# Projections and self-attention as one program: head loads in the last projection steps, fills in free banks

## The reference

```python
q = _ln(latents, sa_ln_g, sa_ln_b)
x = latents + _mha(q, q, sa_in_w, sa_in_b, sa_out_w, sa_out_b)
qc = _ln(x, ca_q_ln_g, ca_q_ln_b)
kv = _ln(tokens, ca_kv_ln_g, ca_kv_ln_b)
x = x + _mha(qc, kv, ca_in_w, ca_in_b, ca_out_w, ca_out_b)
return _fuse_moe(x, moe_ln_g, moe_ln_b, router_w, router_b, e_fc1_w, e_fc1_b, e_fc2_w, e_fc2_b)
...
scores = jnp.einsum('bhqd,bhkd->bhqk', q, k) / jnp.sqrt(jnp.float32(dh))
attn = jax.nn.softmax(scores, axis=-1)
out = jnp.einsum('bhqk,bhkd->bhqd', attn, v)
```

## Time and profile before

| | |
|---|---|
| median of three runs | 1690.89 us (1687.65 to 1694.73) |
| profiled execution | 1686.37 us, span of its trace 1684.6 us |
| projections | 0 to about 139 us |
| self-attention | about 139 to 829 us |
| busy share of the span | PE 86%, DVE 70%, ACT 50%, POOL 44% |

### The profile page before, as it was taken

The page is one execution under the profiler, slowest core; times in us unless marked ns, Lnnn a source line. Parts: engine busy times, 40 slices in busy tenths (PEclk is TensorE's granted clock), DMA queues, the critical chain, the costliest instruction groups (busy, mean ns, idle before and its releaser), DMA issues. The chain is left out here.

```text
span 1684.6 us, 29075 instructions
## 1 busy us (share of the span) xinstructions
PE 1441.5 (86%) x9973; PEld 745.6 (44%) x9974; DVE 1181.5 (70%) x1725; ACT 844.1 (50%) x1709; POOL 743.7 (44%) x465
## 2 busy tenths in 40 slices
PE   5993999999999999999658888873299999999996
PEld 3550222222222222222233544442288888888885
DVE  4755999999999999997165777434655665655653
ACT  2330788888888888888414545340022222222221
POOL 1003999999930000000131221100158887888884
PEclk8995899999999999999876979565599999999999
DMA  3556645574522111200264665535722332333331
GB/s 119 188 212 177 163 132 153 156 215 134 157 57 84 32 32 33 84 1 2 89 142 105 163 140 98 121 73 191 297 42 55 56 55 48 53 60 54 54 57 16
DMA packets 134790, 172.68 MB, mean 103 GB/s; under 512 B 30008, under 2 KB 100089, under 8 KB 134187
## 3 DMA queue, kind: packets, MB, share of 16 engines
q1 hardware_dynamic: 107499, 119.26, 26.6%
q0 software_dynamic: 27200, 52.24, 12.9%
HBM read 102.09 MB, written 66.25 MB: 100 GB/s over the span
## 5 line engine op out<-in xcount | busy, mean ns | idle before, releaser
L1093 DVE TENSOR_REDUCE sa_half_maxs<-sa_psm 128x2 f32<-128x1024 f32 x512 | 604.7, 1221 | 49.7 <-PE sa_psm L961 41.2
L1077 ACT ACTIVATE sa_p<-sa_pss 128x512 f32<-128x512 f32 x1024 | 533.0, 603 | 89.8 <-PE sa_pss L1004 89.6
L1004 PE MATMUL sa_pss<-sa_q,sa_k 49*128 49x512 f16 x1024 | 312.2, 385 | 7.8
L1019 PE MATMUL sa_pso<-sa_p,sa_v 128*32 128x512 f32 x2048 | 273.8, 606 | 18.8 <-ACT sa_o L1055 9.4
L961 PE MATMUL sa_psm<-sa_k,sa_q 48*128 48x512 f16 x1024 | 260.9, 395 | 30.5 <-DMA sa_k<-dram_sa_qk_parts 19.2
L2295 ACT ACTIVATE moe_h<-moe_psh,moe_b 128x256 f32<-128x256 f32 x312 | 122.4, 475 | 328.4 <-PE moe_psh L2232 328.4
L1004 PEld LDWEIGHTS sa_pss<-sa_q,sa_k 49*128 49x128 f16 x1024 | 77.7, 94 | 320.2 <-ACT sa_p L1077 264.9
L1366 POOL TENSOR_TENSOR x_xb<-x_xb,early_bo 128x1024 f32<-128x1024 f32 x4 | 9.4, 2350 | 373.4 <-DMA x_xb<-in_x 373.4
L2231 PE MATMUL moe_psh<-moe_hl,w_high 128*128 128x256 f16 x624 | 171.0, 274 | 0.0
L2230 PE MATMUL moe_psh<-moe_hh,w_high 128*128 128x256 f16 x624 | 170.9, 274 | 0.0
L2232 PE MATMUL moe_psh<-moe_hh,w_low 128*128 128x256 f16 x624 | 170.9, 274 | 0.0
(11 more groups left out here) (205 smaller groups left out, 2026.2 us busy)
## 6 DMA issues: line engine op xcount, KB each, us to landing
sa_w_stage<-in_w POOLq DMA_DIRECT2D x32, 512.0 KB, 5.3
dram_sa_v<-qkv_v_sb SPq DMA_DIRECT2D x8, 1024.0 KB, 5.0
dram_sa_qk_parts<-qkv_part SPq DMA_DIRECT2D x16, 512.0 KB, 6.0
sa_v<-dram_sa_v SPq DMA_DIRECT2D x16, 512.0 KB, 6.5
dram_w_high<-sa_w_high POOLq DMA_DIRECT2D x32, 256.0 KB, 2.8
dram_w_low<-sa_w_low POOLq DMA_DIRECT2D x32, 256.0 KB, 3.6
dram_sa_raw<-sa_o SPq DMA_DIRECT2D x4, 2048.0 KB, 9.1
w_high<-dram_w_high SPq DMA_DIRECT2D x16, 512.0 KB, 14.9
```

What stands on the lines that cost most here:

```text
L1004: pe.matmul(ps_s[place % SBANKS][:], k_st[u][rows, j0 + j, kt * kp:(kt + 1) * kp], q_st[u][rows, j0 + j, half * HALF:(half + 1) * HALF], s ...
L1019: mm = pe.matmul(ps_o[h * VW:(h + 1) * VW, :], v_st[u][:, kt, v_at:v_at + VW], probs[n % PSLOTS][h][:], start=(kt == 0), stop=(kt == key_t ...
L1077: act.activation(probs[n % PSLOTS][h][:], ps_s[place % SBANKS][:], ACT.Exp, scale=float(DH) ** -0.5).then_inc(read, 1)
L1093: dv.tensor_reduce(half_maxs[U % 2][:, at % 2, :, c], ps_m[z][:], AX_X, ALU.max).then_inc(taken, 1)
```

## The change

Projections and self-attention become one block (`front_phase`) with one set of semaphores. The buffers of loads 0 and 1 lie outside the memory that the projections give back; those of loads 2 and 3, the probabilities and the outputs are put in that memory later. SP issues load 0 in step 7 of the x program, behind the stores of block 5, and load 1 in step 8, behind those of block 6; in step 7 it first waits for the stores of blocks 0 and 1, the rows of the first batch. The bank pairs are laid out so that fill 0 goes to the pair that the projections leave free, and fill 1 to the pair of the transposes. When SP has seen all stores of a program land, it raises `over`; PE waits for it ahead of the first turn, ACT ahead of the first exponential, and GpSimd ahead of its first weight piece.

```diff
--- before.py
+++ after.py
@@ -346,6 +347,14 @@
                     sp.dma_start(qk[2][n].rearrange("(c p) n -> p c n", p=P)[
                         :, :, bass.ds(number(i, u) * W, W)], part[n][u][:]
                     ).then_inc(parts_stored[u], 16)
+            if ahead and has(0) and not has(1):
+
+                for u in range(2):
+                    sp.wait_ge(parts_stored[u], 16 * PARTS)
+                    sp.wait_ge(v_stored[u], 16)
+                ahead(sp, 0)
+            if ahead and has(-1) and not has(0):
+                ahead(sp, 1)
         steps(sp, step)
...
+        sp.sem_inc(over, 1)
...
-def tokens_phase(nc, *programs):
...
+def front_phase(nc, early, programs, q_parts, k_parts, v_dram, **attention):
+
+    slots, load_heads, key_tiles = 4, HG, SEQ // P
...
+        heads = [head_buffers(sb, u) for u in range(2)]
...
+        def load(sp, L):
+
+            u = L % slots
+            q_st, k_st, v_st = heads[u]
...
+        block = ctx.enter_context(nc.Block())
+        with ExitStack() as tctx:
+            psum = {"read": {}}
+            made = [tokens_program(nc, tctx, sem, block, psum, *args, **options, over=over,
+                                   ahead=load if n == len(programs) - 1 else None)
+                    for n, (args, options) in enumerate(programs)]
             for stage in range(2):
                 for program in made:
                     next(program, None)
+        with ExitStack() as actx:
...
+            heads += [head_buffers(late, u) for u in range(2, slots)]
+            attention_program(nc, actx, sem, block, "sa", heads, load, loaded, v_loaded, half_maxs, maxs, max_row,
+                              over, len(programs), early=early, **attention)
...
-        ps_s = [ps(f"pss{z}", [kp, HALF]) for z in range(SBANKS)]
-        ps_m = [ps(f"psm{z}", [P, 2, 512]) for z in range(2)]
-        ps_o = ps("pso", [P, HALF])
...
+    ps_m1 = ps("psm1", [P, 2, 512])
+    ps_s = [ps(f"pss{z}", [kp, HALF]) for z in range(SBANKS)]
+    ps_o = ps("pso", [P, HALF])
+    ps_m = [ps("psm0", [P, 2, 512]), ps_m1]
...
-                sp.dma_start(ident[:], ident_dram).then_inc(consts, 16)
-                load(0)
-                for u in range(slots):
...
-                load(1)
-                place_row(0)
...
+        pool.wait_ge(over, programs)
+        pool.wait_ge(filled, 1)
...
+        for n in range(lead):
+            advance(n)
+            if n == fills:
+                pe.wait_ge(consts, 16)
+                pe.wait_ge(over, programs)
+                turn(0)
...
+        keep_row(0)
+        act.wait_ge(over, programs)
```

More of the change, by code:

```diff
@@ L60, in semaphores, with tokens_program @@
     nc.all_engine_barrier()
-def tokens_program(nc, ctx, block, psum, name, x_dram, rows, blocks, *, ln_g, ln_b, ident_dram,
-                   attn=None, qk=None, v=None, router=None, weights=None):
+def tokens_program(nc, ctx, make_sem, block, psum, name, x_dram, rows, blocks, *, ln_g, ln_b, ident_dram,
+                   attn=None, qk=None, v=None, router=None, weights=None, ahead=None, over=None):
     W = TPB * rows
@@ L657, in early_buffers, with attention_program @@
     return made
-def attention_phase(nc, name, q_parts, k_parts, v_dram, raw_dram, ident_dram, ones_dram, weights, w_cut, early,
-                    a, ck_parts, cv_dram, r1):
+def attention_program(nc, ctx, sem, block, name, heads, load, loaded, v_loaded, half_maxs, maxs, max_row, over,
+                      programs, early, raw_dram, ident_dram, ones_dram, weights, w_cut, a, ck_parts, cv_dram, r1):
     keys = SEQ
@@ new lines, in attention_program @@
+    taken = sem("taken")
+    joined = sem("joined")
+    row_placed = [sem(f"row_placed{z}") for z in range(2)]
+    in_bank = sem("in_bank")
+    read = sem("read")
+    weighted = sem("weighted")
+    o_taken = sem("o_taken")
+    stored = [sem(f"stored{e}") for e in range(2)]
+    w_loaded = [sem(f"w_loaded{z}") for z in range(STAGES)]
+    w_highs = sem("w_highs")
+    w_scaled = sem("w_scaled")
+    w_lows = sem("w_lows")
+    w_stored = [sem(f"w_stored{z}") for z in range(2)]
+    sums_loaded = [sem(f"sums_loaded{b}") for b in range(BATCH - 1)]
@@ new lines, in attention_program, with home, period @@
+    recip_ready, recip_stored = sem("recip_ready"), sem("recip_stored")
+    early_consts, early_x, early_o = sem("early_consts"), sem("early_x"), sem("early_o")
+    EARLY = 16 * (13 + 2 * len(K_STACK) + 2)
+    first_recip = 2 * (batch_groups + 1) * fills + lead
+    LOADS = 16 * 2 * 2 * len(Q_STACK)
+    STORES = 16
+    def home(G):
+        L, g = divmod(G, groups_per_load)
+        return L % slots, g * PAIRS, L // slots
+    def period(n):
+        G, bt = divmod(n, per_group)
+        half, kt = divmod(bt, key_tiles)
+        return G, half, kt
@@ new lines, in _, with take, join @@
+    @block.vector
+    def _(dv):
+        def take(n):
+            U, f = divmod(n, fills)
+            z = n % 2
+            dv.wait_ge(filled, n + 1)
+            j, at = divmod(f, q_tiles)
+            c = j * q_tiles // 2 + at // 2
+            dv.tensor_reduce(half_maxs[U % 2][:, at % 2, :, c], ps_m[z][:], AX_X, ALU.max
+                             ).then_inc(taken, 1)
+        def join(U):
+            dv.wait_ge(taken, (U + 1) * fills)
+            if U >= 2:
+                dv.wait_ge(in_bank, row_place(U - 2) + 1)
+            dv.tensor_tensor(maxs[U % 2][:], half_maxs[U % 2][:, 0], half_maxs[U % 2][:, 1],
+                             ALU.max).then_inc(joined, 1)
+        for n in range(all_fills + 1):
+            U, f = divmod(n, fills)
+            if f == 0 and n > 0:
+                join(U - 1)
+            if n < all_fills:
+                take(n)
+            if n == first_recip:
+                dv.wait_ge(sums_loaded[0], 16)
+                dv.reciprocal(early["recips1"][:, 0, :], early["sums1"][:, 0, :]).then_inc(recip_ready, 1)
```

688 lines of the change are left out of this document (315 added, 373 removed).

## The result

The changed kernel takes 1679.57 us (median of 17 runs, 1669.91 to 1683.62) against 1690.89 (17 runs) of the kernel before: 0.9921 of its time, 95% interval 0.9904 to 0.9939, which is 10 to 16 us less. The profiled execution took 1682.22 us, its span 1680.4. The forecast of 1672.6 had the sign and the mechanism; the gain is some two thirds of the 18.3 us.

A forecast was written before the change was run, and what follows sets the result against it. It took the kernel as a line of phases, each starting when the one ahead ends, with the vector engine idle 18.32 us at the seam. Only the seam's 18.3 us counted, other terms 0: 1672.6 from the median 1690.89; range 1665 to 1680.

The forecast's parts named there:

- The seam, -18.3: Between projections and self-attention: first maximum starts when block 7 is evacuated, at 130.55 instead of 148.87, 18.3 us earlier.
- Load 0, 0 to 0.3: Load 0 in step 7, behind block 5's stores: 6.0 us of issue, landed in time; cost 0 to 0.3 us, taken as 0.
- Load 1, 0: Load 1 in step 8: block 7's stores land at 142 at the latest, before the first row turn at 148.9; cost 0.
- The lead moves along: Start of self-attention: everything up to the first score moves with the first maxima, 173.47 becoming 155.15.
- GpSimd starts at 137.3 and this gives nothing: GpSimd's weight split starts at about 137.3 instead of 149.16; with hundreds of microseconds to spare, no gain by itself.
- Units of 20.1: Later self-attention: each unit (16 fills, 32 scores) keeps its pace of 20.1 us, as its instructions stay unchanged.
- the rival of slower units: Self-attention: other banks and buffer addresses lengthen each unit; at 0.8 us a unit the time is 1698.2; chance 0.04.
- The end of the program, 0: End of the new merged program: it clears its semaphores once, as the old attention did; cost 0.
- The clock stays up: Rival in the lead: PE's clock survives it, worth up to 2.6 us more, giving 1670.0; chance 0.14.
- The first row late: Rival: GpSimd's stores and a load delay the first row copies and first score by up to 2.7 us, 1675.3; chance 0.10.
- Only half of the change takes effect: Rival at the seam: first fill or maximum still held until `over`; gain 10.9 us, time 1680.0; chance 0.06.
- The sum: Whole kernel: profiled execution 1686.37 less 18.3 gives 1668.1; the same change on the median 1690.89 gives 1672.6.

The follow-up runs named there:

- the split in step: Changed kernel, with each pair of GpSimd's weight-split pieces waiting for one join of the maxima: 1678.98 us (12 runs) against 1677.93 (6).

## Why the prediction was right, and where its sizes were off

- *The seam, -18.3.* Right: -18.6 in the mean of the profiles, the first maximum at the end of block 7's evacuation in all four. The run without early loads shows that 2 of it belong to the removed program end and 16.5 to the loads.
- *Load 0, 0 to 0.3.* Right: the first fill waits for nothing. Its issue took 8.3 us instead of the 6.0 that I carried over, the first three issues 0.75 to 1.22 us each amid block 5's stores; the cover, until 128.56, was long enough.
- *Load 1, 0.* Right on the time: the stores land at 142, the far end that I had written down, with 6 us left to the first row's turn. But taking it out was not neutral, by way of GpSimd.
- *The lead moves along.* Right: 24.63 against 24.60.
- *GpSimd starts at 137.3 and this gives nothing.* This step failed. I had let the stores land at 142 in the paragraph ahead and still started GpSimd at the old moment; it starts at 142.2 to 142.9. And its place against the joins is not free: self-attention is 1.9 us longer from the first join on, of which the split in step gives back 1.1 in one profile. Another 0.5 is the longer first unit, which no term of the prediction had.
- *Units of 20.1.* Right for the pace (20.06 to 20.12), and the rival of slower units fell. What is added sits in three or four units a profile, which a mean pace from joins of units 8 to 31 does not show. The prediction took from these rows that GpSimd beside them hardly touches the pace; its own rows 1 held a join of 0.96 us for the usual 0.18.
- *The end of the program, 0.* Off by 0.8: from the last evacuation to cross-attention 8.8 us in place of 8.0, in every profile. The cause was not followed.
- *The clock stays up* (0.14). Fell: 0.50 from 136, as before the change; the first wait of the scores is unchanged and the second longer (0.83 for 0.24). The Trainium skill (TensorE: Matmul & The Clock Gate, "A second HAM failure mode: psum-queue depth-cycling"), which I set against this rival, puts such a fall down to short idles between groups of matmuls. The traces agree as far as they go: the clock fell with idles of 2.2 and then 0.74 us ahead of the fills, and stood until 156 in the run that filled them from the third fill on. What it takes to come back is another matter: in two runs it was 0.50 at 4.00 of 4 us busy.
- *The first row late* (0.10). It did not happen here: 24.63 us, and 2.8 us from the last copy's issue to the first score. Late copies beside GpSimd's stores do occur, as in the run with load 1 late (4.3 us, beside stores at 149.81); GpSimd's later start, which I had wrong, kept them off the first row.
- *Only half of the change takes effect* (0.06). By the time alone this rival's 1680.0 is nearer to the measured 1679.57 than the forecast is. The trace rules it out: neither the first fill nor the first maximum waits for `over`.
- *The sum.* 1668.1 for that execution against 1682.22; by medians 11.3 us of gain for 18.3, by 33 runs 13.4. The profiles close the account: 18.6 at the seam, less 1.9 in self-attention, 0.8 at its end and 2.0 in the expert layer, is 13.9. The first two losses stand in every profile and are the change's; the third lies inside what single executions differ by. The measured 1679.57 lies 0.4 us below the upper end of my range, 1680, which I had set for a first fill that waits and not for these losses: that it lies inside is in part luck.

## What to carry to other kernels

Let the next stage's first loads go out as soon as their data have landed, and let its first instructions wait for just those: of this seam 16.5 us were the loads and 2 the end of the program with its barrier. When a seam moves, look at what else changes its place against the critical engine: an engine with hundreds of microseconds to spare can still stretch short operations that share something with it, and a second trace of each kernel shows what is scatter. Judge a stage by its own events in the trace where the phases behind it differ by 10 us between executions.

## What the runs showed of the hardware

A GpSimd operation on SBUF holds up the vector engine's operation with two inputs in SBUF (a join, 0.17 us), as counted above: for the whole of a GpSimd operation with two inputs (2.1 to 2.4 us), but only to 1.07 us into one with a single input (2.8 us). The Trainium skill (SBUF — State Buffer, "Who interferes with whom") says that a vector instruction with two inputs in SBUF contends with a GpSimd instruction that reads SBUF, that what they share is an exclusive lock, and that the order of issue decides who waits. The traces agree for the two-input case (a join of 2.01 us ended with the operation); in the single-input case the wait ended at 1.07 of 2.8 us, well before the operation. That GpSimd waits in its turn for a join is not shown here. The maxima, which read PSUM, kept their pace of 1.13 us a piece beside GpSimd.

In two runs in which TensorE's clock had already fallen, it stayed at the lower level at 4.00 of 4 us busy: for 25 us on 48-row f16 matmuls, and for 40 us on fills mixed with 128-row f32 matmuls of the kind that went with the upper level in another run.
